# Scale row and second bias rows made inside attention, step means in the first stage, query copies one item later

## What is computed

```python
x = x + attention(ln(x))        # 12 heads of 16, 1024 tokens per image, relative position bias from rel_h, rel_w
t = t + ffn(ln(t))

def ffn(x0):                     # QN, QP = -8, 7
    xq = round(clip(x0 / mean(alpha_a1), QN, QP))
    wq1 = round(clip(w1 / alpha_w1[:, None], QN, QP))
    x1 = clip(gelu((xq @ wq1.T) * alpha_w1 * mean(alpha_a1) + b1), -10, 10)
    hq = round(clip(x1 / mean(alpha_a2), QN, QP))
    wq2 = round(clip(w2 / alpha_w2[:, None], QN, QP))
    return (hq @ wq2.T) * alpha_w2 * mean(alpha_a2) + b2
```

## Time and profile before

| | us |
|---|---|
| median of 3 runs | 850.96 |
| lowest, highest | 850.57, 851.51 |
| the profiled execution | 851.78 |
| its span, first to last instruction | 850.0 |

### The profile page before, as it was taken

The page is one execution under the profiler, slowest core; times in us unless marked ns, Lnnn a source line. Parts: engine busy times, 40 slices in busy tenths (PEclk is TensorE's granted clock), DMA queues, the critical chain, the costliest instruction groups (busy, mean ns, idle before and its releaser), DMA issues. The chain is left out here.

```text
span 850.0 us, 14826 instructions
## 1 busy us (share of the span) xinstructions
PE 766.3 (90%) x5688; PEld 400.5 (47%) x5688; DVE 703.3 (83%) x933; ACT 580.0 (68%) x971; POOL 451.4 (53%) x293
## 2 busy tenths in 40 slices
PE   4998536689999999999999999999999999989975
PEld 2655436444444444444444444444444444357753
DVE  7998897798888888888888888888888887349994
ACT  1334225528777877887788778887878778858773
POOL 5777773368373846557473738465483333412330
PEclk9999768669999999999999999999999999999997
DMA  7686668998768492929487684939295210033411
GB/s 191 200 241 195 210 172 283 367 209 175 140 141 178 99 206 71 212 59 223 90 180 140 130 189 89 202 73 214 63 219 100 96 42 13 13 125 127 154 37 56
DMA packets 65338, 125.91 MB, mean 148 GB/s; under 512 B 9555, under 2 KB 45492, under 8 KB 57324
## 3 DMA queue, kind: packets, MB, share of 16 engines
q1 hardware_dynamic: 57236, 111.84, 56.4%
q10 hardware_dynamic: 8032, 13.13, 4.4%
HBM read 85.53 MB, written 34.60 MB: 141 GB/s over the span
## 5 line engine op out<-in xcount | busy, mean ns | idle before, releaser
L1181 DVE TENSOR_REDUCE at_neg_max<-at_r_ps 128x1 f16<-128x1024 f32 x384 | 451.5, 1217 | 76.3 <-PE at_r_ps L1035 76.3
L1132 ACT ACTIVATE at_probs<-at_s_ps 128x512 f32<-128x512 f32 x768 | 410.9, 600 | 92.5 <-PE at_s_ps L1055 91.6
L1055 PE MATMUL at_s_ps<-op_mix_q,op_mix_k 128*128 128x512 f16 x768 | 264.7, 382 | 4.6 <-ACT at_probs L1132 1.6
L1035 PE MATMUL at_r_ps<-op_mix_k,op_mix_q 128*128 128x256 f16 (+1 forms) x1920 | 238.7, 257 | 9.3 <-PEq L86 4.8
L1067 PE MATMUL at_o_ps<-at_probs,op_v_u 128*32 128x512 f32 x1536 | 204.1, 604 | 0.0
L1035 PEld LDWEIGHTS at_r_ps<-op_mix_k,op_mix_q 128*128 128x128 f16 x1920 | 156.3, 99 | 86.7 <-DVE at_neg_max L1181 15.9
L948 POOL COPY op_mix_q<-op_mix_q 2x4096 f16<-2x4096 f16 x48 | 171.5, 3598 | 1.5
L1055 PEld LDWEIGHTS at_s_ps<-op_mix_q,op_mix_k 128*128 128x128 f16 x768 | 74.1, 97 | 166.3 <-issue 69.6
L227 POOL MEMSET op_mix_q<- 2x10240 f32 x11 | 94.9, 8629 | 21.2 <-PE at_o_ps L1067 21.1
L952 POOL TENSOR_TENSOR at_o_sb<-at_o_sb,at_inv_rows 128x512 f32<-128x512 f32 x23 | 29.5, 1283 | 126.6 <-DVE at_inv_rows L1197 125.4
L945 POOL COPY op_mix_q<-op_mix_q 2x1024 f16<-2x1024 f16 x24 | 24.8, 1034 | 94.6 <-ACT op_mix_q L1137 94.6
(11 more groups left out here) (134 smaller groups left out, 710.6 us busy)
## 6 DMA issues: line engine op xcount, KB each, us to landing
op_mix_q<-qk_parts SPq DMA_DIRECT2D x40, 640.0 KB, 9.5
op_mix_q<-bias_parts SPq DMA_DIRECT2D x120, 120.0 KB, 9.5
op_mix_q<-bias_parts SPq DMA_DIRECT2D x72, 128.0 KB, 9.5
qk_parts<-op_mix_q SPq DMA_DIRECT2D x24, 256.0 KB, 2.4
v_rows<-pr_v_st SPq DMA_DIRECT2D x8, 768.0 KB, 4.1
op_mix_k<-qk_parts SPq DMA_DIRECT2D x48, 128.0 KB, 13.3
op_v_u<-v_rows SPq DMA_DIRECT2D x12, 512.0 KB, 14.1
op_mix_q<-bias_parts SPq DMA_DIRECT2D x24, 256.0 KB, 9.7
```

Source lines behind the costliest of these rows:

```text
L1035: last = pe.matmul(r_ps[count % RRING][:, first // GROUP, first % GROUP:first % GROUP + n], mix_q[owner.buf][:, variant, j, qt * P:(qt + 1 ...
L1055: pe.matmul(s_ps[use % SRING][:, :], mix_k[unit.buf][:, j, keys], mix_q[unit.buf][:, ops.VARIANT_OF[kt], j, queries], start=True, stop=Tru ...
L1132: act.activation(probs[n % PRING][:, j, :], s_ps[use % SRING][:, :], ACT.Exp).then_inc(s_taken, 1)
L1181: dve.tensor_reduce(neg_max[half][:, j // 2, t, j % 2:j % 2 + 1], r_ps[count % RRING][:, :, :].rearrange("p h t -> p (h t)"), AX_X, ALU.ma ...
```

## The change

`scales` is cut up. The two mean steps, their reciprocals, s1 and the four bound instructions (`mean_steps`, `invert_steps`) follow the reciprocals of the first stage, in group 1. The scale row and the two memsets (`scale_rows`), the division of the bias (`divide_bias`) and its three splits (`split_bias`) go into attention: behind the row maxima of steps 12 and 14 of unit 5, and of steps 5, 7 and 12 of unit 6. The bias row has its own load, which SP issues in unit 4, and two new rows of memory. All of it is chained as before. The copies of query 0 in the second stage come one item later: behind items 4 and 5 instead of 3 and 4. SP no longer waits for `scaled` ahead of the rows of zeros, and DVE's copies wait for `quantised`, which is long there. POOL waits for `scaled` at the end of attention.

```diff
...
                     prepare.invert(dve)
+                    prepare.mean_steps(dve)
+                    prepare.invert_steps(dve)
                 if g.last:
                     prepare.quantise(dve, 0)
                     prepare.quantise(dve, 1)
...
     HIGH_LEFT, LOW_LEFT = (7,), (6, 7)
-    SCALES_AFTER, SPREAD_AFTER = 0, {3: (1, 2), 4: (3, 4)}
+    SPREAD_AFTER = {4: (1, 2), 5: (3, 4)}
     with Phase(nc, "rb") as ph:
         q_parts = ops.q_parts
         stage = ops.stage + [ph.sb("stage2", [P, 2, BATCH, SEQ], F16)]
...
             sp.wait_ge(prepare.quantised, 2)
-            sp.wait_ge(prepare.scaled, 1)
             sp.wait_ge(tables.tab_lo, 2 * CHUNKS)
             ops.load_zeros(sp, tables.parity)
             sp.wait_ge(ops.image0_stored, IMAGE0)
...
                     last.then_inc(lo_done, 1)
-                if i == SCALES_AFTER:
-                    prep.scales(dve)
                 if i in SPREAD_AFTER:
                     dve.wait_ge(ops.q_in[0], 16 * 4)
-                    dve.wait_ge(prep.scaled, 1)
+                    dve.wait_ge(prep.quantised, 2)
                     dve.wait_ge(tables.tab_lo, 2 * CHUNKS)
                     for variant in SPREAD_AFTER[i]:
                         dve.tensor_copy(ops.variant_of_q(0, variant), ops.variant_of_q(0, 0)).then_inc(ops.q_spread[0], 1)
...
     Q_BY_ACT, Q_BY_POOL = (1, 2), (3, 4)
+    SCALES_IN = 5
     with Phase(nc, "at") as ph:
         mix_q, mix_k, v_u, ident16 = ops.mix_q, ops.mix_k, ops.v_u, ops.ident16
         MAX_ROW, TILE_ORDER = ops.MAX_ROW, ops.TILE_ORDER
...
         o_ps = ph.ps("o_ps", [P, GROUP], F32)
+        wt.place_scales(ph)
...
             each_unit(pool, emit)
+            pool.wait_ge(wt.scaled, 1)
             ffn_in.inverse_std(pool, FIRST, wt.inv_a1)
...
                 store(unit, 0)
+                if unit.u == SCALES_IN - 1:
+                    wt.load_bias(sp)
...
                             invert(owner, half)
+                    if unit.u == SCALES_IN:
+                        if n == 12:
+                            wt.scale_rows(dve)
+                        if n == 14:
+                            wt.divide_bias(dve)
+                    if unit.u == SCALES_IN + 1 and n in (5, 7, 12):
+                        wt.split_bias(dve, (5, 7, 12).index(n))
                     if unit.last and n == HEAD_AT:
                         ffn_in.residual(dve, FIRST, p_ps)
                         ffn_in.normalise(dve, FIRST)
...
             self.sem(n) for n in ("zeroed", "ident_made", "params_in", "chained", "turned", "copied", "quantised"))
-        self.links, self.scaled = 0, self.sem("scaled")
+        self.links, self.scaled, self.bias_in = 0, self.sem("scaled"), self.sem("bias_in")
         self.aw2_sb, self.inv_w2 = self.sb("aw2_sb", [HALF, 2], F32), self.sb("inv_w2", [HALF, 2], F32)
...
-        area, lens = ops.weight_area, (HT * C, HID, C, HT, HT, C, C)
+        area, lens = ops.weight_area, (HT * C, HID, C, HT, HT)
         assert sum(lens) <= area.shape[1]
         places = []
         for n in lens:
             places.append(area[:, 0:n])
             area = area[:, n:]
         self.w1_f = places[0].rearrange("p (t c) -> p t c", c=C)
-        self.aa2_row, self.aa1_row, self.aw1_sb, self.inv_w1, self.b2_row, self.inv_s2 = places[1:7]
-        self.b2_high = self.inv_s2.bitcast(BF16)[:, 0:C]
+        self.aa2_row, self.aa1_row, self.aw1_sb, self.inv_w1 = places[1:5]
         self.w2_f = ops.spare[0:HALF, 0:2 * HID].rearrange("p (h c) -> p h c", h=2)
         wide1, wide2 = (v[:, :, :, :].bitcast(BF16).rearrange("p k h e -> p (k h e)") for v in ops.v_u[1:])
         self.w1_q = wide1[:, 0:HT * C].rearrange("p (t c) -> p t c", c=C)
...
+    def place_scales(self, ph):
+        rows = ph.sb("scale_rows", [P, 2 * C], F32)
+        self.b2_row, self.inv_s2 = rows[:, 0:C], rows[:, C:2 * C]
+        self.b2_high = self.inv_s2.bitcast(BF16)[:, 0:C]
     def pool(self, pool):
         make_identity(pool, self.ident, self.zeroed, self.ident_made)
...
                          (self.aw1_sb[:, :], aw1), (self.aw2_sb[:, :], aw2_cols), (self.s2_row[:, :], aw2.partition_broadcast(P)),
-                         (self.aa1_row[:, :], aa1.partition_broadcast(P)), (self.aa2_row[:, :], aa2.partition_broadcast(P)),
-                         (self.b2_row[:, :], b2.partition_broadcast(P))):
+                         (self.aa1_row[:, :], aa1.partition_broadcast(P)), (self.aa2_row[:, :], aa2.partition_broadcast(P))):
             sp.dma_start(dst, src).then_inc(self.params_in, 16)
+    def load_bias(self, sp):
+        sp.dma_start(self.b2_row, self.dram[7].partition_broadcast(P)).then_inc(self.bias_in, 16)
...
-        dve.wait_ge(self.params_in, 16 * 8)
+        dve.wait_ge(self.params_in, 16 * 7)
         self.chain(dve, dve.reciprocal(self.inv_w1[:, :], self.aw1_sb[:, :]))
         self.chain(dve, dve.reciprocal(self.inv_w2[:, :], self.aw2_sb[:, :]))
...
-    def scales(self, dve):
-        step, link = self.step, lambda ins: self.chain(dve, ins)
...
+    def mean_steps(self, dve):
+        self.chain(dve, dve.tensor_reduce(self.step[:, 0:1], self.aa1_row[:, :], AX_X, ALU.add))
+        self.chain(dve, dve.tensor_reduce(self.step[:, 1:2], self.aa2_row[:, :], AX_X, ALU.add))
+        self.chain(dve, dve.tensor_scalar(self.step[:, 2:3], self.step[:, 0:1], 1.0 / C, None, ALU.mult))
+        self.chain(dve, dve.tensor_scalar(self.step[:, 3:4], self.step[:, 1:2], 1.0 / HID, None, ALU.mult))
+    def invert_steps(self, dve):
+        self.chain(dve, dve.reciprocal(self.step[:, 4:6], self.step[:, 2:4]))
+        self.chain(dve, dve.tensor_scalar(self.s1[:, :], self.aw1_sb[:, :], self.step[:, 2:3], None, ALU.mult))
         for at, edge, limit, op in ((0, 10.0, QP, ALU.min), (1, -10.0, QN, ALU.max)):
-            link(dve.tensor_scalar(self.bound[:, at:at + 1], self.inv_a2, edge, MAGIC, ALU.mult, ALU.add))
-            last = dve.tensor_scalar(self.bound[:, 2 + at:3 + at], self.bound[:, at:at + 1], MAGIC + limit, None, op)
-        last.then_inc(self.scaled, 1)
+            self.chain(dve, dve.tensor_scalar(self.bound[:, at:at + 1], self.inv_a2, edge, MAGIC, ALU.mult, ALU.add))
+            self.chain(dve, dve.tensor_scalar(self.bound[:, 2 + at:3 + at], self.bound[:, at:at + 1], MAGIC + limit, None, op))
+    def scale_rows(self, dve):
+        self.chain(dve, dve.tensor_scalar(self.s2_row[:, :], self.s2_row[:, :], self.step[:, 3:4], None, ALU.mult))
+        self.chain(dve, dve.memset(self.b2_parts[:, :], 0.0))
+        self.chain(dve, dve.memset(self.ones[:, :], 1.0))
+    def divide_bias(self, dve):
+        dve.wait_ge(self.bias_in, 16)
+        self.chain(dve, dve.reciprocal(self.inv_s2, self.s2_row[:, :]))
+        self.chain(dve, dve.tensor_tensor(self.b2_row, self.b2_row, self.inv_s2, ALU.mult))
+    def split_bias(self, dve, i):
+        row = slice(i * SLOT, i * SLOT + 1)
+        self.chain(dve, dve.tensor_scalar(self.b2_high, self.b2_row, 1.0, None, ALU.mult))
+        self.chain(dve, dve.tensor_scalar(self.b2_parts[row, :], self.b2_high[row, :], 1.0, None, ALU.mult))
+        if i < 2:
+            self.chain(dve, dve.tensor_tensor(self.b2_row, self.b2_row, self.b2_high, ALU.subtract))
+        else:
+            dve.nop().then_inc(self.scaled, 1)
...
```

17 lines of the change are left out of this document (removed).

## The result

The kernel after takes 853.62 us (median of 8, 852.48 to 856.1), the kernel before on the same chip 850.85 (median of 8). The ratio is 1.0032, with a 95% interval of 1.002 to 1.0043: slower by 2.8 us, where 848.7 and faster was forecast. The profiled execution took 853.50, its span 851.7; that of before 851.78, and 850.0.

A forecast was written before the change was run, and what follows sets the result against it. DVE was taken to bound the first stage, a PE-ACT-DVE chain the second, PE attention. 3.0 - 9.4 + 4.1 = -2.3 on the median of 850.96 gave 848.7 us, range 844.5 to 851.7 (8 in 10).

The forecast's parts named there:

- First stage, +3.0: First stage: ten more instructions on DVE, its bound, cost 3.0 us in full, with 2.5 to 3.2 as bounds.
- Second stage, -9.4: Second stage: without the block of scales, chunk 9 and items 2 and 3 come 9.9 us earlier; net gain 9.4.
- What is late next: End of second stage: DVE's own copies end last, close behind them SP's bias and query loads; 0.6 us taken off.
- the bounds, 10.2 and 7: Second stage's gain: 10.2 us if the loads keep pace, 7 if they fall 3 us behind.
- rival (c): Second stage: its end stays tied to the loads, gain 7 instead of 9.4, 851.1 us; chance 0.15.
- Attention, +4.1: Attention: two DVE instructions wait for POOL's running copies, so PE waits 1.4 and 2.7 us, 4.1 in all.
- Rival (a): Attention: POOL's copies don't hold DVE, so it costs only 0.35 us, 844.9 in all; chance 0.17.
- Rival (b), the clock in the long wait: Attention: PE's clock falls in the 2.7 us wait, costing 1.35 us, 850.1 in all; chance 0.12.
- Rival (d): Attention: the product waits through both POOL copies, 3.57 us more, and the clock falls after each wait; 855.0 us, chance 0.06.

The follow-up runs named there:

- e5: e2 with the ten mean and bound instructions moved from the first stage into DVE's idle time in the second, SP's zeros behind them: 848.02 us, 0.9956 of before.
- e1: The kernel after, with the two loads of the rows of zeros issued behind the wait for item 1's first stores: 855.37 us, 1.0051 of before.
- e10: e2 with the hot rows and zeros loaded behind item 0's bias loads instead of ahead of them: 854.45 us, 1.0038 of before.
- e13: The kernel after, with the hot rows issued ahead of the second stage's first query, key and value loads: 850.95 us, 1.0 of before.
- e2: The kernel after, with the attention pieces moved to steps where POOL is idle and the division cut in two: 849.31 us, 0.9974 of before.
- e8: The kernel after, with the third split moved from step 12 of unit 6 to step 7 of unit 7, beside POOL's copy: 856.82 us, 1.0074 of before.

## Why the prediction was wrong, point by point

- **First stage, +3.0: right.** 2.97 for the ten instructions, 3.2 at the stage's end. e5 gave it back there. But as a term of the whole it was too plain: of the 3.2 that e5 starts earlier only 1.3 arrive at attention.
- **Second stage, -9.4: wrong, and the step that failed.** It was the step from "ACT issues item 1's stores for 3.8 us" to chunk 9 at 123.45, 9.9 us earlier. The issues took 9.2. In the old clock chunk 9 came at 130.64 - 3.2 = 127.4, 5.9 before the 133.30 of the earlier trace rows, and 5.9 is what attention gained. The 3.8 was taken from the earlier trace rows, from a time in which the DMA engines stood half idle, and carried to a time in which the hot rows and zeros were being worked off; there it is 9.2. The text saw that backlog, and took off 0.6 for it. In the scales' removal the zeros' wait for `scaled` went as well, so they moved ahead of the stores. e1 puts 3.0 of the 5.4 us in the issues to that (with the spread between executions, 1 to 3), and e10 and e13 show that without a backlog of hot rows the issues are as short as forecast.
- **What is late next.** Named were DVE's copies and, close behind, SP. DVE's copies did end the stage, at 159.20, SP at 157.72. But the bounds, 10.2 and 7, did not reach far enough: their lower end, like rival (c), allowed only for late loads, and ACT's issues were taken as sure. Rival (c) had a gain of 7 because the stage stays tied to the loads; 5.9 was gained, and in the kernel after it was the chain of ACT and DVE that held it. The tie to the loads is real, as e13 and e5 show, and comes out once that chain is short: SP's 22 loads, 26.2 us before and after, then take 30 to 32 us. Why they take longer isn't shown: the DMA share of 1.0 that the earlier trace rows show for 140 to 160 reaches back to 115 there, but nearly so in after too.
- **Attention, +4.1: right,** 4.3 measured, from 1.59 and 3.32 us for the two held instructions; PE's waits were 1.1 and 2.3 where 1.4 and 2.7 were forecast. The trace agrees with the rule of the Trainium skill that was weighed there ("SBUF — State Buffer", "Who interferes with whom"): the cast took 3.32 beside a copy of two partitions and 0.25 without, and the reductions ran on beside the copies. Rival (a) fell with it. Its near-zero cost is had only where POOL is idle, as e2 shows.
- **Rival (b), the clock in the long wait: in some executions.** It did not fall in the profile of after, and did in those of e13 and e8, for 1.36, where the forecast had 1.35. With a chance of 0.12 it was taken for a property of the kernel, and it changes from one execution to the next.
- **Rival (d)** did not come: the product waited for the end of the running copy, not through both.
- **The whole.** 3.2 - 5.9 + 4.3 = 1.6 in place of 3.0 - 9.4 + 4.1 = -2.3. 3.5 of the 3.9 us between them are the second stage. The medians are 2.8 apart, of which the profiles account for 1.7; 0.93 lies in that the profiled execution of before was above its median, and 0.1 in that after's was below. What sets the medians that much further apart than the profiles isn't shown; falls of the clock in other executions than the profiled ones are one candidate. The range ended at 851.7. With 5.9 in place of 9.4 its own sum gives 850.96 + 3.0 - 5.9 + 4.1 = 852.2, outside it: the second stage's lower bound of 7 was too high.
